# Four products in four PSUM banks, narrow products, and unread products in the edge layers of a four-layer graph kernel

## The chip, the cores and the metric

The kernel runs on one core of a Trainium2 chip. The core has a matrix engine (PE), a vector engine (DVE), a scalar engine (ACT), a general engine (POOL, which here issues the gathers), and SP, which issues DMAs. The metric is the device time of one execution in microseconds, the median of several runs. PE's granted clock is given as a share of 2.4 GHz: a stretch shows a mean between 0.5 (1.2 GHz) and 1.0.

## What is computed

A graph of 100,000 nodes with 16 features each and 50,000 edges goes through four layers. `h` is the layer norm of `x` with a relu, `src` and `dst` the ends of the edges:

```python
h = relu(layernorm(x)); x = x + L0(h)   # messages h[src] * edge weight * w0, summed by dst
h = relu(layernorm(x)); x = x + L1(h)   # msg = sum_k t[:, k] * (h[dst] @ W[k]), 16 terms, summed by src
h = relu(layernorm(x)); x = x + L2(h)   # two edge convolutions, 16 inputs x 8 outputs x 9 edge terms each
                                        # (two own layer norms), plus h @ Wr + bias for every node ("root")
h = relu(layernorm(x)); x = x + L3(h)   # m = silu(einsum('ei,ej,ijh->eh', h[dst], attr8, Wmsg)) @ Wlin, summed by src;
                                        # then for every node silu(einsum('ni,nh,ihk->nk', h, agg, Wupd)) @ Wulin + h
```

## The kernel before

The edges are first sorted by block of nodes (a block is 14 columns of nodes) into records in DRAM, once by `dst` (`edges_by_dst`) and once by `src` (`edges_by_src`); POOL writes them with `place`. A layer's edges are 448 tiles of 128 edges, 8 tiles make a group (`G`), so a layer has 56 groups; in the code a group is `group(i, k)`, `g = i * RING + k`, with four buffers for rows and records (`RING`). A node stage between layers adds the sums to `x` and writes the next `h` to a table. At the end seven chunks of an update work through all nodes.

What happens to a group `g` in layers 1, 2 and 3:

- SP fetches its records, POOL gathers its rows of the table (8 indirect DMAs, line 464, one for each tile).
- PE transposes the rows (line 587), ACT copies the transpose to `featT` (line 780; in layer 2 twice, with two gains, line 777). In `featT` the 8 tiles' 16 features lie in 8 bands of 16 partitions.
- PE multiplies `featT` by a block-diagonal weight matrix: four products in layers 1 (512 columns) and 2 (288 columns), two in layer 3 (512 columns), at line 560. Each product concerns only two tiles (32 partitions) in layer 1 and four tiles (64 partitions) in layers 2 and 3; the other rows of its columns are zeros. Two PSUM banks, `psP`, take the products in turn, so product 2 waits for DVE's multiplication 0 and product 3 for multiplication 1.
- DVE multiplies each product by the edge's terms (lines 1155, 1168, 1183), reduces (1160, 1176, 1188), and spreads the messages over the columns of their block (`spread_out`, line 1112). In layer 2, PE also computes the "root" products of a part of the nodes (line 576), DVE waits for them before it reduces, as they lie in the bank where it writes, and adds them to `x` at the group's end (1212, 1214).
- PE sums the edges of group `g - 1` by node: eight products, one for each tile, of 224 columns (line 551), into `psK`, 4 banks of two tiles each. DVE adds them up in a running sum (`run`, line 1130), eight steps, each with the one before as input. The sums come in halves of four: DVE waits for four, PE for the running sums of the same tiles of the group before.
- SP writes the running sums to DRAM (`keep_run`) and fetches the records for group `g + 4`.

PE executes in the order in which the code is written: transpose, four products, (root products), eight sums of the group before. In layer 1, six products that nobody reads (`ident` times part of `W3`, line 595) stand between products 1 and 2. Layer 0 has no products; DVE scales the rows (1139, 1143).

DVE's order in a group is: the terms and the block columns (1148, 1107), the multiplications, the reduction, the spreading, the running sums of the group before. In layer 3 the running sums stand before the spreading, while ACT computes the silu.

In the update (line 653) PE makes, for each quad of nodes, two products of 512 columns in the two halves of `psQ[q % 2]`; DVE multiplies them (1265) and reduces what POOL has halved (1258, 495). Three times a chunk PE also transposes or multiplies for the chunk's other steps (618, 624, 630). A float32 product shows as two records of MATMUL in the trace.

Of the kernel before, what the change touches and what calls it, by code (L numbers as in the profile page):

```python
# [4 lines left out]
P = 128  # L5
# [67 lines left out]
def build_gnn(nc, x_in, src_in, dst_in, attr2_in, attr8_in, attr8_rev_in, ew_in, w0_in, slw_in, w1_in,  # L73
# [10 lines left out]
    with ctx:  # L84
# [118 lines left out]
        psR = psX[:, 1536:2048]  # L203
        raw = [psR[:, 256 + i * P:256 + (i + 1) * P] for i in range(2)]
# [297 lines left out]
        def _(pe):  # L502
# [22 lines left out]

            for l in range(4):
# [3 lines left out]
                if l == 1:  # L530
                    parts = [(0, W1[:, m * 512:(m + 1) * 512]) for m in range(4)]
                elif l == 2:
                    parts = [(s, W2[s][:, q * 288:(q + 1) * 288]) for s in range(2) for q in range(2)]
                elif l == 3:
                    parts = [(0, W3[:, m * 512:(m + 1) * 512]) for m in range(2)]
                else:
                    parts = []
                n = len(parts)

                def sums(i, k, half, first=False):  # L540

                    q = i * RING + (k - 1)
                    par = (k - 1) % 2
# [5 lines left out]
                    for t in range(4 * half, 4 * half + 4):  # L549
                        o = t // 2 * 512 + t % 2 * BW  # L550
                        nc.tensor.matmul(psK[:, o:o + BW], at_lo[par][:, t * P:(t + 1) * P],  # L551
                                         spread[par][:, t * BW:(t + 1) * BW], start=True, stop=True)\
                            .then_inc(e["summed"], 1)

                def product(i, k, m, first):
                    g = i * RING + k
                    s, w = parts[m]
                    if m >= 2 or not first:
                        pe.wait_ge(e["used"], g * n + (m - 1))
                    nc.tensor.matmul(psP[m % 2][:, 0:w.shape[1]], featT[:, s * P:(s + 1) * P], w,  # L560
# [20 lines left out]
                def group(i, k, first=False, second=False):  # L581
                    g = i * RING + k
                    if l:
# [6 lines left out]
                        for m in range(n):  # L590
                            product(i, k, m, first)
                            if l == 1 and m == 1:

                                for _ in range(6):
                                    nc.tensor.matmul(psT[:, 256:512], ident[:, :], W3[:, 0:256], start=True, stop=True)
                        if l == 2:
                            root_products(i, k, first)
                    if not first:
                        sums(i, k, 0, second)
                        sums(i, k, 1, second)  # L600

# [32 lines left out]
            def step(c, first, last_one):  # L634
                for q in range(QUADS):
# [15 lines left out]
                    for j in range(2):  # L651
                        b, m = q // 2, 2 * (q % 2) + j
                        k = nc.tensor.matmul(psQ[q % 2][:, j * 512:(j + 1) * 512], rt[:, b * P:(b + 1) * P],  # L653
# [662 lines left out]
```

## Time and profile before

| | us |
|---|---|
| median of 3 runs | 4295.58 |
| lowest and highest | 4289.64, 4299.15 |
| the profiled execution | 4291.38 |
| its span on the core | 4289.6 |

The profile gives the busy time of each engine, the idle time of an engine before an instruction with what ended it ("waited for"), and the chain of work that ended last. "issue" is time in which an engine waited for nothing that the profile shows. In the table by stage the engines' busy times come first, with their counts of instructions, then PE's granted clock, the share of DMA time and GB/s. PEld is PE's loading of weights. In a row of the trace an operation is named by its line, its kind, what it writes and reads, and the number of instructions merged in the row ("x16"); behind it in brackets stands the idle time before it and what ended it. Names drop the numbers of buffers.

### The profile page before, as it was taken

Reading aid. Unit: us, or ns where it says so; the run is one execution under the profiler, and the core shown is the slowest. Engines: PE = TensorE matmul, PEld = TensorE weight load, DVE = VectorE, ACT = ScalarE, POOL = GpSimd, SP = SyncE. Lnnn points to the kernel's source line nnn. Section 1 sums busy time; section 2 is a strip of 40 time slices with the busy share of each in tenths; the row PEclk is TensorE's granted clock in tenths of the full one; section 3 lists DMA queues with packets and bytes.
Section 4 is the critical chain, followed back from the end, with each engine's and each line's share of the span. In section 5 each row is a group of like instructions: output and inputs, shape, how many; then the busy total and the mean of one; then the engine's idle time right before and its main releaser. Section 6 shows DMA issues by size and latency. Waiting matters only on the chain.

```text
span 4289.6 us, 28738 instructions
## 1 busy us (share of the span) xinstructions
PE 2171.9 (51%) x7442; PEld 1517.8 (35%) x7442; DVE 2886.2 (67%) x4329; ACT 1192.7 (28%) x2949; POOL 2739.8 (64%) x2799
## 2 busy tenths in 40 slices
PE   1200035545300005888887046667651666767998
PEld 1100024444300003555555035555540444444444
DVE  8892036666570005888888867777767888877887
ACT  1000023333420003333343234444422433430110
POOL 3777777777777777655653056666622777764776
PEclk7555567777655557999999568888875888889999
DMA  6011023333630001222223322222343333351110
GB/s 178 9 31 46 8 59 109 110 102 109 101 101 5 5 5 45 83 83 79 87 83 86 98 69 91 90 89 83 90 95 111 107 98 107 107 95 43 35 35 26
DMA packets 200521, 321.19 MB, mean 75 GB/s; under 512 B 83898, under 2 KB 166698, under 8 KB 199971
## 3 DMA queue, kind: packets, MB, share of 16 engines
q1 hardware_dynamic: 112848, 265.61, 17.3%
q0 software_dynamic: 82368, 21.64, 7.7%
q10 hardware_dynamic: 5140, 32.09, 2.0%
q8 instruction: 60, 0.98, 0.1%
q14 instruction: 105, 0.86, 0.1%
HBM read 66.90 MB, written 252.21 MB: 74 GB/s over the span
## 4 chain that ended last, share of the span: by engine, by line
POOL 38%; DVE 23%; issue 19%; PE 17%; DMA 1%; SPq 1%; ACT 0%; DVEq 0%; POOLq 0%
POOL rows L464 20%; DVE work L1130 9%; POOL edges_by_dst L448 9%; POOL edges_by_src L448 9%; PE psX L653 7%; PE psX L560 6%; DVE psX L1160 3%; DVE natD L1155 2%; DVE psX L1176 2%; PE psX L576 2%; DVE h L1020 1%; PE psK L551 1%; DVE psX L1017 1%; PE psK L630 1%; DVE x L1214 0%
## 5 line engine op out<-in xcount | busy, mean ns | idle before, releaser
L464 POOL DMA_INDIRECT rows<-table,rec x1792 | 1693.0, 945 | 1087.1 <-issue 519.2
L551 PE MATMUL psK<-work 128*128 128x224 f32 x3584 | 896.1, 413 | 576.5 <-DVE work L1112 298.1
L551 PEld LDWEIGHTS psK<-work 128*128 128x128 f32 x3584 | 822.1, 234 | 719.7 <-issue 666.4
L1130 DVE SCALAR_TENSOR_TENSOR work<-work,keep,psK 128x224 f32<-128x224 f32 x1792 | 800.9, 447 | 87.3 <-PE psK L551 15.9
L560 PE MATMUL psX<-natD 128*128 128x512 f32 (+1 forms) x1120 | 608.4, 678 | 340.4 <-DVE natD L1168 150.0
L760 ACT ACTIVATE work<-iota,rec 128x128 f32<-128x128 f32 x1792 | 545.9, 391 | 576.2 <-PE psK L551 358.9
L448 POOL DMA_INDIRECT edges_by_dst<-natD,pos x391 | 374.7, 958 | 184.2 <-issue 127.0
L1112 DVE TENSOR_TENSOR work<-at_hi,psX 128x1792 f32<-128x1792 f32 x224 | 452.2, 2019 | 6.1 <-ACT psX L802 0.3
L448 POOL DMA_INDIRECT edges_by_src<-natS,pos x391 | 374.4, 958 | 128.1 <-issue 128.1
L587 PE MATMUL psX<-ident,rows 128*128 128x128 f32 x168 | 51.6, 307 | 767.3 <-DMA rows<-table,rec 767.3
L560 PEld LDWEIGHTS psX<-natD 128*128 128x128 f32 x1120 | 231.4, 229 | 556.5 <-DVE natD L1168 176.3
L653 PE MATMUL psX<-natD,work 128*128 128x512 f32 x784 | 339.9, 592 | 1.0 <-ACT work L838 1.0
L495 POOL TENSOR_TENSOR work<-natS 128x512 f32<-128x512 f32 x196 | 244.6, 1262 | 129.7 <-DVE natS L1265 129.4
L780 ACT ACTIVATE natD<-psX 128x128 f32<-128x128 f32 x112 | 31.1, 278 | 1048.8 <-PE psX L587 1048.8
L587 PEld LDWEIGHTS psX<-ident,rows 128*128 128x128 f32 x168 | 24.3, 145 | 790.1 <-issue 496.8
L1139 DVE TENSOR_TENSOR psX<-rows,rec 128x128 f32<-128x128 f32 x56 | 17.0, 303 | 426.3 <-DMA rows<-table,rec 426.3
L1265 DVE TENSOR_TENSOR natS<-psX,h 128x1024 f32<-128x1024 f32 x196 | 237.9, 1214 | 56.0 <-PE psX L653 56.0
L1148 DVE TENSOR_TENSOR natD<-hats 128x128 f32<-128x128 f32 x56 | 15.9, 284 | 379.6 <-ACT hats L751 379.6
L764 ACT ACTIVATE work<-work,one 128x1024 f32<-128x1024 f32 x224 | 257.1, 1148 | 7.3
L653 PEld LDWEIGHTS psX<-natD,work 128*128 128x128 f32 x784 | 145.0, 189 | 182.4 <-issue 109.8
L1155 DVE TENSOR_TENSOR natD<-psX,natD 128x512 f32<-128x512 f32 x224 | 149.7, 689 | 77.5 <-PE psX L560 75.6
L1168 DVE TENSOR_TENSOR natD<-psX,rec 128x288 f32<-128x288 f32 x224 | 97.1, 453 | 92.4 <-PE psX L560 92.2
(147 smaller groups left out, 2342.6 us busy)
## 6 DMA issues: line engine op xcount, KB each, us to landing
scan<-work SPq DMA_DIRECT2D x224, 896.0 KB
rows<-table,rec POOLq DMA_INDIRECT x1792
table<-h ACTq DMA_DIRECT2D x28, 896.0 KB, 3.6
work<-scan SPq DMA_DIRECT2D x168, 112.0 KB, 2.0
rec<-edges_by_dst SPq DMA_DIRECT2D x112, 84.0 KB, 1.9
natD<-scan SPq DMA_DIRECT2D x56, 112.0 KB, 2.0
edges_by_dst<-natD,pos POOLq DMA_INDIRECT x391
edges_by_src<-natS,pos POOLq DMA_INDIRECT x391
```

Source lines behind the costliest of these rows:

```text
L448: pool.indirect_dma_start(out=rec_by[s].ap(), out_offset=bass.IndirectOffsetOnAxis(ap=pos[s][0:n, u:u + 1], axis=0), in_=nat[0:n, u * F:(u ...
L464: pool.indirect_dma_start(out=rows[k][:, u * D:(u + 1) * D], out_offset=None, in_=table.ap(), in_offset=bass.IndirectOffsetOnAxis(ap=rec[k ...
L495: nc.gpsimd.tensor_tensor(hf, w[:, :, :, 0:8], w[:, :, :, 8:16], ALU.add).then_inc(up["half"], 1)
L551: nc.tensor.matmul(psK[:, o:o + BW], at_lo[par][:, t * P:(t + 1) * P], spread[par][:, t * BW:(t + 1) * BW], start=True, stop=True)\
L560: nc.tensor.matmul(psP[m % 2][:, 0:w.shape[1]], featT[:, s * P:(s + 1) * P], w, start=True, stop=True).then_inc(e["prod"], 1)
L653: k = nc.tensor.matmul(psQ[q % 2][:, j * 512:(j + 1) * 512], rt[:, b * P:(b + 1) * P], W4[:, m * 512:(m + 1) * 512], start=True, stop=True)
L760: a = S.activation(at_lo[par][:, t * P:(t + 1) * P], iota1[:, :], ACT.Abs, bias=field(l, k, LO[ORDER[l]])[:, t, :])
L764: S.activation(at_lo[par], at_lo[par], ACT.Relu, scale=-1.0, bias=one[:, :]).then_inc(e["lo"], 1)
L1112: V.tensor_tensor(spread[par].rearrange("p (u c f) -> p u c f", c=BC, f=D), v3(at_hi[par][:, :], BC)[:, :, :, None].to_broadcast([P, G, BC ...
L1130: V.scalar_tensor_tensor(acc[par][:, t * BW:(t + 1) * BW], was, keep[s][:, bass.ds(q * G + t, 1)], psK[:, o:o + BW], ALU.mult, ALU.add).th ...
L1155: V.tensor_tensor(prod[:, m * 512:(m + 1) * 512].rearrange("p (u o k) -> p u o k", o=D, k=D), psP[m % 2].rearrange("p (u o k) -> p u o k", ...
L1265: V.tensor_tensor(products(q)[0], psQ[q % 2].rearrange("p (u k i) -> p u k i", k=D, i=D), v3(h[:, bass.ds(c * CW + 64 * q, 64)])[:, :, Non ...
```

## The change

Four things are done.

1. In layers 1 and 2 products 2 and 3 go to the first two banks of `psK` (where the sums of tiles 0 to 3 lie) instead of `psP`. On PE the sums of tiles 4 to 7 now stand before those of tiles 0 to 3, and the latter wait, two by two, for DVE's multiplications 2 and 3. In layer 2 the root products stand between the two halves. DVE's running sums wait once for all eight sums in these two layers.
2. Each product reads only the partitions of `featT` and of the weights that count: 32 in layer 1, 64 in layers 2 and 3, and 32 in the final update.
3. Unread products (`spin`): four in layer 1, at the end of a group instead of six between products; four between the halves of the sums and six behind them in layers 0 and 3. Layer 2 has none.
4. Product 0 and 1 of a group wait for multiplications 0 and 1 of the group before.

```diff
+        product_at = psP + [psK[:, 0:512], psK[:, 512:1024]]
...
+            def spin(n):
+                for _ in range(n):
+                    nc.tensor.matmul(psT[:, 256:512], ident[:, :], keep[0][:, 0:256], start=True, stop=True)
...
-                    parts = [(0, W1[:, m * 512:(m + 1) * 512]) for m in range(4)]
+                    parts = [(0, 32 * m, 32, W1[:, m * 512:(m + 1) * 512]) for m in range(4)]
...
-                    parts = [(s, W2[s][:, q * 288:(q + 1) * 288]) for s in range(2) for q in range(2)]
+                    parts = [(s, 64 * q, 64, W2[s][:, q * 288:(q + 1) * 288]) for s in range(2) for q in range(2)]
...
-                    parts = [(0, W3[:, m * 512:(m + 1) * 512]) for m in range(2)]
+                    parts = [(0, 64 * m, 64, W3[:, m * 512:(m + 1) * 512]) for m in range(2)]
...
+                def late_product(g, m):
+                    s, row, high, w = parts[m]
+                    if g == 1:
+                        pe.wait_ge(e["used"], m + 1)
+                    elif g > 1:
+                        pe.wait_ge(e["run"], (g - 2) * G + 2 * (m - 1))
+                    nc.tensor.matmul(psK[:, (m - 2) * 512:(m - 2) * 512 + w.shape[1]],
+                                     featT[row:row + high, s * P:(s + 1) * P], w[row:row + high, :],
+                                     start=True, stop=True).then_inc(e["prod"], 1)
+                def upper_sums(g):
+                    pe.wait_ge(e["spread"], g)
+                    pe.wait_ge(e["lo"], g)
+                    if g > 1:
+                        pe.wait_ge(e["run"], (g - 1) * G)
+                    sums_of(g - 1, range(4, 8))
+                def lower_sums(g):
+                    for b in range(2):
+                        pe.wait_ge(e["used"], g * n + 3 + b)
+                        sums_of(g - 1, (2 * b, 2 * b + 1))
...
-                    if m >= 2 or not first:
-                        pe.wait_ge(e["used"], g * n + (m - 1))
+                    if not first:
+                        pe.wait_ge(e["used"], (g - 1) * n + (m + 1))
...
-                        for m in range(n):
+                        for m in range(2):
                             product(i, k, m, first)
-                            if l == 1 and m == 1:
-                                for _ in range(6):
-                                    nc.tensor.matmul(psT[:, 256:512], ident[:, :], W3[:, 0:256], start=True, stop=True)
+                    if n == 4:
+                        for m in range(2, 4):
+                            late_product(g, m)
+                        if not first:
+                            upper_sums(g)
                         if l == 2:
                             root_products(i, k, first)
-                    if not first:
+                        if not first:
+                            lower_sums(g)
+                        if l == 1:
+                            spin(4)
+                    elif not first:
                         sums(i, k, 0, second)
+                        spin(4)
                         sums(i, k, 1, second)
+                        spin(6)
...
-                        k = nc.tensor.matmul(psQ[q % 2][:, j * 512:(j + 1) * 512], rt[:, b * P:(b + 1) * P],
-                                             W4[:, m * 512:(m + 1) * 512], start=True, stop=True)
+                        two = slice(32 * m, 32 * m + 32)
+                        k = nc.tensor.matmul(psQ[q % 2][:, j * 512:(j + 1) * 512], rt[two, b * P:(b + 1) * P],
+                                             W4[two, m * 512:(m + 1) * 512], start=True, stop=True)
...
-                        if t % 4 == 0:
+                        if l in (1, 2):
+                            if t == 0:
+                                dve.wait_ge(e["summed"], q * G + G)
+                        elif t % 4 == 0:
                             dve.wait_ge(e["summed"], q * G + (t + 4))
```

DVE's multiplications read `product_at[m]` instead of `psP[m % 2]`.

PE in layer 1, one group in the middle of the layer, before. `psK<-work` are the sums, `psX<-natD` the products, `ident` with 256 columns the unread ones; in brackets the semaphores that a row waits for (`used` counts DVE's multiplications, `run` its running sums).

```order
L587 MATMUL psX<-ident,rows 128x128 [waits gath3]
L560 MATMUL psX<-natD 128x512 [waits e1_used,e1_bandS]
L560 MATMUL psX<-natD 128x512 [waits e1_used]
L595 MATMUL psX<-natD,ident 128x256 x6
L560 MATMUL psX<-natD 128x512 [waits e1_used] x2
L551 MATMUL psK<-work 128x224 [waits e1_run,e1_lo,e1_spread]
L551 MATMUL psK<-work 128x224 x3
L551 MATMUL psK<-work 128x224 [waits e1_run]
L551 MATMUL psK<-work 128x224 x3
```

The same group's place in the changed kernel:

```order
L623 MATMUL psX<-ident,rows 128x128 [waits gath0]
L595 MATMUL psX<-natD 128x512 [waits e1_used,e1_bandS]
L595 MATMUL psX<-natD 128x512 [waits e1_used]
L571 MATMUL psK<-natD 128x512 [waits e1_run] x2
L550 MATMUL psK<-work 128x224 [waits e1_run,e1_lo,e1_spread]
L550 MATMUL psK<-work 128x224 x3
L550 MATMUL psK<-work 128x224 [waits e1_used]
L550 MATMUL psK<-work 128x224
L550 MATMUL psK<-work 128x224 [waits e1_used]
L550 MATMUL psK<-work 128x224
L530 MATMUL psX<-keep,ident 128x256 x4
```

The wait for `used` has moved from products 2 and 3 to the last four sums, and products 2 and 3 wait for `run`.

PE in layer 2, one group before (`root` products are the 128 x 128 ones behind the products):

```order
L587 MATMUL psX<-ident,rows 128x128
L560 MATMUL psX<-natD 128x288 [waits e2_used,e2_bandS]
L560 MATMUL psX<-natD 128x288 [waits e2_used] x3
L576 MATMUL psX<-natD 128x128 [waits r_added,r_rowsS]
L576 MATMUL psX<-natD 128x128 x3
L551 MATMUL psK<-work 128x224 [waits e2_run,e2_lo,e2_spread]
L551 MATMUL psK<-work 128x224 x3
L551 MATMUL psK<-work 128x224 [waits e2_run]
L551 MATMUL psK<-work 128x224 x3
```

And in the changed kernel:

```order
L623 MATMUL psX<-ident,rows 128x128
L595 MATMUL psX<-natD 128x288 [waits e2_used,e2_bandS]
L595 MATMUL psX<-natD 128x288 [waits e2_used]
L571 MATMUL psK<-natD 128x288 [waits e2_run] x2
L550 MATMUL psK<-work 128x224 [waits e2_run,e2_lo,e2_spread]
L550 MATMUL psK<-work 128x224 x3
L612 MATMUL psX<-natD 128x128 [waits r_added,r_rowsS]
L612 MATMUL psX<-natD 128x128 x3
L550 MATMUL psK<-work 128x224 [waits e2_used]
L550 MATMUL psK<-work 128x224
L550 MATMUL psK<-work 128x224 [waits e2_used]
L550 MATMUL psK<-work 128x224
```

The root products now follow four sums, which wait for the end of the running sums before.

## Rows read from the trace of the kernel before

**Rows 1.** The page: the chain that ended last, by engine and by line.

```profile
POOL 38%; DVE 23%; issue 19%; PE 17%; DMA 1%; SPq 1%; ACT 0%; DVEq 0%; POOLq 0%
POOL rows L464 20%; DVE work L1130 9%; POOL edges_by_dst L448 9%; POOL edges_by_src L448 9%; PE psX L653 7%; PE psX L560 6%; DVE psX L1160 3%; DVE natD L1155 2%; DVE psX L1176 2%; PE psX L576 2%; DVE h L1020 1%; PE psK L551 1%; DVE psX L1017 1%; PE psK L630 1%; DVE x L1214 0%
```

**Rows 2.** Layers 0 to 3, update: PE, PEld, DVE, ACT, POOL busy (x); PEclk, DMA.

```profile
580.00:1137.00 557.00, 288.98 (x880) 248.87 (x880) 336.10 (x652) 204.14 (x522) 421.39 (x446) 0.72 0.39 103
1645.00:2350.00 705.00, 581.18 (x2065) 397.59 (x2064) 605.62 (x890) 274.19 (x835) 412.58 (x438) 0.94 0.28 80
2518.00:3187.00 669.00, 465.74 (x1871) 385.38 (x1871) 523.76 (x997) 297.50 (x769) 407.64 (x431) 0.81 0.31 88
3301.00:3874.00 573.00, 383.09 (x1171) 254.09 (x1171) 458.59 (x726) 223.33 (x607) 411.09 (x436) 0.83 0.37 100
3888.00:4284.00 396.00, 385.57 (x1176) 193.55 (x1176) 342.08 (x393) 47.67 (x41) 295.26 (x209) 0.98 0.10 28
```

**Rows 3.** Who waited for whom in layer 1: us, times, longest.

```profile
DVE natD L1155 <- PE psX L560: 75.6, 114, 3.1
```

**Rows 4.** Layer 1's first operation of a group on DVE: ns, first and last start.

```profile
L1148 DVE TENSOR_TENSOR natD<-hats x56: 282/283/293, 1645.2 to 2336.8; 128x128 f32<-128x128 f32 x56
```

**Rows 5.** Timeline of layer 1: start, duration, operation, [idle time before it].

```profile
2066.95 3.19 PE L551 MATMUL psK<-work 128*128 128x224 f32 x16
...
2072.44 2.75 PE L595 MATMUL psX<-natD,ident 128*128 128x256 f32 x12
...
2077.20 2.50 PE L560 MATMUL psX<-natD 128*128 128x512 f32 x4 [2.01 <-DVE natD L1155]
...
2079.74 0.69 DVE L1155 TENSOR_TENSOR natD<-psX,natD 128x512 f32<-128x512 f32 x1 [0.69 <-PE psX L560]
...
2084.73 3.89 DVE L1130 SCALAR_TENSOR_TENSOR work<-work,keep,psK 128x224 f32<-128x224 f32 x8
```

**Rows 6.** Who waited for whom in layer 2.

```profile
DVE natD L1168 <- PE psX L560: 72.7, 103, 1.1
...
DVE psX L1176 <- PE psX L576: 50.6, 55, 1.3
```

**Rows 7.** Layer 2's reductions on DVE, two a group.

```profile
L1176 DVE TENSOR_REDUCE psX<-natD x112: 748/756/761, 2515.7 to 3178.1; 128x64 f32<-128x576 f32 x112
```

**Rows 8.** Timeline of layer 2, two groups one after the other.

```profile
2702.21 1.24 PE L560 MATMUL psX<-natD 128*128 128x288 f32 x4 [1.66 <-DVE natD L1168]
...
2703.28 1.05 PE L576 MATMUL psX<-natD 128*128 128x128 f32 x8
...
2704.44 1.42 DVE L1176 TENSOR_REDUCE psX<-natD 128x64 f32<-128x576 f32 x2 [0.50 <-PE psX L576]
...
2707.83 3.89 DVE L1130 SCALAR_TENSOR_TENSOR work<-work,keep,psK 128x224 f32<-128x224 f32 x8
...
2713.12 2.04 PE L560 MATMUL psX<-natD 128*128 128x288 f32 x4 [3.29 <-DVE natD L1168]
...
2716.97 1.42 DVE L1176 TENSOR_REDUCE psX<-natD 128x64 f32<-128x576 f32 x2 [1.32 <-PE psX L576]
```

**Rows 9.** Timeline of layer 3, POOL: two gathers, eight apart.

```profile
3520.28 0.94 POOL L464 DMA_INDIRECT rows<-table,rec  x1 [0.30 <-issue]
...
3530.26 0.94 POOL L464 DMA_INDIRECT rows<-table,rec  x1 [0.30 <-issue]
```

**Rows 10.** Who waited for whom in the final update.

```profile
DVE natS L1265 <- PE psX L653: 56.0, 22, 20.3
```

**Rows 11.** The chain of work in the update: start, us, engine and line.

```profile
3974.03 30.91 PE psX L653 x72
...
4028.30 30.91 PE psX L653 x72
```

**Rows 12.** Timeline of the update, DVE: two multiplications, one quad apart.

```profile
4031.79 1.21 DVE L1265 TENSOR_TENSOR natS<-psX,h 128x1024 f32<-128x1024 f32 x1
...
4033.51 1.21 DVE L1265 TENSOR_TENSOR natS<-psX,h 128x1024 f32<-128x1024 f32 x1
```

More of the change, by code:

```diff
@@ L538, in _, with sums_of @@
                 n = len(parts)
+                def sums_of(q, tiles):
+                    par = q % 2
+                    for t in tiles:
+                        o = t // 2 * 512 + t % 2 * BW
+                        nc.tensor.matmul(psK[:, o:o + BW], at_lo[par][:, t * P:(t + 1) * P],
+                                         spread[par][:, t * BW:(t + 1) * BW], start=True, stop=True)\
+                            .then_inc(e["summed"], 1)
                 def sums(i, k, half, first=False):
                     q = i * RING + (k - 1)
-                    par = (k - 1) % 2
                     if half == 0:
@@ L548, in sums @@
                         pe.wait_ge(e["run"], q * G + (4 * half + 4 - G))
[L549 to L553, printed above, removed]
+                    sums_of(q, range(4 * half, 4 * half + 4))
+                def late_product(g, m):
[17 more added lines that the diff above has]
+                        sums_of(g - 1, (2 * b, 2 * b + 1))
                 def product(i, k, m, first):
                     g = i * RING + k
-                    s, w = parts[m]
-                    if m >= 2 or not first:
-                        pe.wait_ge(e["used"], g * n + (m - 1))
-                    nc.tensor.matmul(psP[m % 2][:, 0:w.shape[1]], featT[:, s * P:(s + 1) * P], w,
+                    s, row, high, w = parts[m]
+                    if not first:
+                        pe.wait_ge(e["used"], (g - 1) * n + (m + 1))
+                    nc.tensor.matmul(psP[m % 2][:, 0:w.shape[1]], featT[row:row + high, s * P:(s + 1) * P],
+                                     w[row:row + high, :],
                                      start=True, stop=True).then_inc(e["prod"], 1)
@@ L1155, in messages @@
                             V.tensor_tensor(prod[:, m * 512:(m + 1) * 512].rearrange("p (u o k) -> p u o k", o=D, k=D),
-                                            psP[m % 2].rearrange("p (u o k) -> p u o k", o=D, k=D),
+                                            product_at[m].rearrange("p (u o k) -> p u o k", o=D, k=D),
                                             v3(basis)[:, 2 * m:2 * m + 2, None, :].to_broadcast([P, 2, D, D]),
@@ L1169, in messages @@
                                             .rearrange("p (u o t) -> p u o t", o=HALF, t=A9),
-                                            psP[m % 2][:, 0:288].rearrange("p (u o t) -> p u o t", o=HALF, t=A9),
+                                            product_at[m][:, 0:288].rearrange("p (u o t) -> p u o t", o=HALF, t=A9),
                                             at.to_broadcast([P, 4, HALF, A9]), ALU.mult).then_inc(e["used"], 1)
```

## The prediction

> **What bounds the kernel now.** I read the chain of work first [rows 1]: POOL holds 38% of it, DVE 23%, PE 17%, so no one engine is the kernel's limit and each stage has to be read alone. The busy time by stage [rows 2] gives five stretches: layer 0's edges, layers 1, 2 and 3's edges, and the final update. What is left out between them (sorting, placing edges, node stages) the change doesn't touch.
>
> Layer 1. A group takes 12.57 us (the first operation of a group runs 56 times from 1645.2 to 2336.8: 691.6 / 55) [rows 4]. DVE is busy 86% of the stretch, POOL 59% [rows 2]. DVE's only large wait is for products, 75.6 us [rows 3], less 3 us or so at the first group, 1.31 us a group. One group shows it [rows 5]: product 2 may not start before DVE has freed the bank of product 0, so PE stands idle 2.01 us, issues products 2 and 3 at 2077.20, and DVE idles before each of its last two multiplications, 0.69 us before the last. Without the waits a group is 12.57 - 1.31 = 11.26 us of DVE work.
>
> Layer 2. A group takes 12.03 us: its two reductions run from 2515.7 to 3178.1, less 0.7 us between the two of a group, over 55 [rows 7]. DVE waits 72.7 us for products and 50.6 us for the root sums that stand behind them on PE [rows 6], together 2.24 us a group, which leaves 9.79 us. The clock has a part in it: the stretch ran at 0.81 of full speed, so about 38% of the time at 1.2 GHz and the rest at 2.4 [rows 2]. PE idled 3.29 us before products 2 and 3, they then ran at half speed (2.04 us, against 1.24 at full speed in the group before), and DVE waited 1.32 us for the root sums, against 0.50 us in that group before [rows 8].
>
> Layers 0 and 3. POOL issues gathers without a break: eight of them, one group, from 3520.28 to 3530.26, so 9.98 us [rows 9]. It is POOL that sets these layers, at 0.72 and 0.83 of PE's clock [rows 2]; behind layer 0, POOL goes on with placing edges by source (9% of the chain) [rows 1], for which no other engine is needed.
>
> Final update. PE is on the chain: 72 products' records in 30.91 us, 0.429 us each, 1.72 us for the four of a quad, and between them bursts for transposes and the step's small products; a chunk takes 4028.30 - 3974.03 = 54.27 us [rows 11]. DVE's own pace is the same 1.72 us a quad with no idle time between [rows 12], 28 x 1.72 = 48.2 us a chunk, so the other 6 us are DVE's waits: 56.0 us in all, 20.3 of them the first one [rows 10], leaving 36 us.
>
> **The change, part by part.**
>
> *Products 2 and 3 in other banks, layer 1.* They no longer wait for multiplications 0 and 1 of the same group but for the running sums of tiles 0 to 3 of two groups back, which end on DVE before the group begins. So all four products should lie ready, and 1.31 us a group goes. What is late next: the sums of tiles 0 to 3 now stand behind multiplications 2 and 3, and DVE waits for all eight sums where it waited for four and four. That wait has cover: the reduction and the spreading lie between, and in the group shown 2084.73 - 2079.74 = 5.0 us pass from the start of multiplication 3 to the first running sum [rows 5], while the lower four sums take about 1.5 us at 2.4 GHz (half of the 3.19 us of all eight [rows 5]) and under 3.5 at 1.2. Behind PE's waits are queued only its own next sums and, after them, the next group's transpose, wanted some 7 us later. ACT's columns and SP's refills wait for counts that come no later than now. Bounds: 73 us (56 x 1.31) and, should half of the waits come back through a slower clock, 37. I take a period of 11.35 us, near the first end because the work left on PE fits: 56 x (12.57 - 11.35) = **-68 us**.
>
> *The same in layer 2.* Products 2 and 3 leave the multiplications' shadow, and the root products now stand behind the upper four sums, which wait for the end of the previous running sums. From the end of the running sums PE then needs, at full clock, 1.6 us for four sums (half of 3.19 [rows 5]) and 1.05 us for the root products [rows 8], 2.65 us. DVE is busy meanwhile with the root additions, the block columns and four multiplications: of its 9.79 us a group the reductions, the spreading and the running sums take 2707.83 + 3.89 - 2704.44 = 7.28 [rows 8], so 2.5 us are left for these. So 0.1 to 0.4 us of the 2.24 stay at 2.4 GHz (0.4 where the group before had fewer root blocks to add); at 1.2 GHz PE's 2.65 become 5.3, and some 2.5 us stay. DVE without idle time is 9.79 us, POOL 9.98 us: POOL becomes the floor. For the clock: PE's longest gap is now 3.29 us, in layer 1 it is 2.01, and that layer ran at 0.94 against 0.81 [rows 2, 5, 8]. In the new order I find PE's gaps (waiting for tile pairs, for the end of the run, for multiplications) at 1.5 us or less, so a clock like layer 1's. Bounds: a period of 10.0 us gives 56 x 2.03 = 114 us; the clock staying at 0.81 gives about 10.9 us (38% of the groups with 2.5 us, the others with 0.3), 63. I take 10.35: 56 x 1.68 = **-94 us**.
>
> *Unread products.* Layer 1 goes from six to four, in a place where PE waits anyway: nothing. Layers 0 and 3 get ten a group. Six take 2.75 us at full clock [rows 5], ten 4.6. In layer 0 they come to eight sums (about 3.0 us): 7.6 of 9.98 us, hidden by POOL's gathers. In layer 3 it is tight: sums, transpose, copy and two products take 2072.44 - 2066.95 = 5.49 us, ten unread products about 4.35 us back to back: 9.84 us against POOL's 9.98 [rows 5, 9]. If the clock drops as in layer 1 (0.94) it is some 10.4 us, +0.4 x 56 = 24 us. Bounds 0 and +30; I take **+5 us**, since a PE without idle time ran at the full clock in the final stage (0.98) [rows 2].
>
> *Products that read only 32 or 64 rows.* No row shows such a product at work beside another. If it streams as long as now, nothing changes; if two of a quad overlap, PE ceases to bind the update and DVE's pace stays, at most -36 us [rows 10, 12]. The bursts remain (54.27 - 28 x 1.72 = 6.1 us a chunk), and DVE would still wait at some. I take **-15 us**, between the ends and nearer to none, since nothing in the rows shows an overlap. By a page of the Trainium skill (TensorE: Matmul & The Clock Gate, Part 3) products whose operands start in different row groups run concurrently, four of 32 rows measured at 3.07 times the speed; by that the term would be -20 to -36. No run here shows it yet. Against the change speaks another page (TensorEngine Tiling (Array Packing), Key Properties): a change of tiling mode drains TensorE. Each group of layers 1 to 3 would have two changes; at 0.17 us each, an estimate from the time by which a pair of products lasts longer than the distance to what follows it (1.24 against 2703.28 - 2702.21 = 1.07 us [rows 8]), they would be hidden in layers 1 and 2 and would take layer 3 from 9.84 to 10.18 us, +11 us.
>
> *DVE, ACT, POOL, SP* execute the same instructions, except for fewer waits: nothing.
>
> **Sum.** -68 - 94 + 5 - 15 = -172 us. The profiled execution took 4291.4 us (span 4289.6), so 4119.4; it lies 4.2 us under the median of 4295.6, so 4124 for the median.
>
> **Rivals.**
>
> A. *The narrow products gain nothing, and layer 3 turns to PE.* For it: no row shows an overlap, and layer 3's margin is 0.14 us a group. Time: the update term 0, layer 3 +20: 4124 + 15 + 15 = 4154. It is also the case in which this part of the change doesn't do what it says.
>
> B. *The clock doesn't recover.* Layer 2 stays near 0.81 and its root sums stay late: -63 instead of -94, layer 1 -50 instead of -68: 4124 + 49 = 4173. For it: the share of time in which PE streams falls if products overlap. Against it: the gaps get shorter.
>
> C. *Slower than before.* PE's clock in the final update falls from full to half, because PE works on a quarter of its rows or because overlapped products leave it idle half the time. Its place is the 196 quads, where 1.72 us of PE work would be 3.43: 196 x 1.71 = 335 us, and without the 15 us gained there, 4124 + 15 + 335 = about 4474. It turns slower than before when the update loses more than the 157 us that the layers gain, 157 / 196 = 0.80 us a quad, so at a mean clock under about 0.7 there. Against it: the stretch is at 0.98 with PE the limit [rows 2], and a PE that becomes slow becomes busy again.
>
> **How the numbers follow.** Forecast case 0.60, centre 4124, with its own unknowns from 4124 - 20 (layer 2 at 10.0) - 21 (update at full gain) = about 4083 up to 4160. A 0.20, B 0.12, C 0.05, others 0.03. To hold eight times in ten the range takes in A and B and the errors about them: 4080 to 4200. A difference under 0.2% (8.6 us) is about what a measurement of this kernel can't tell from none. Faster by more: all of the forecast, A and B and most of the rest, 0.93; the same 0.02; slower 0.05.
>
> **What would show it.** In the new profile: DVE's wait for products in layer 1 near zero and its group at 11.3 us; DVE's wait for root sums in layer 2 under 0.5 us a group, the stretch's clock at 0.9 or more, POOL without waits for records; layer 3's group still 10 us with PE near 100% busy at clock 1.0; in the update, a chunk of 50 to 52 us and PE below 90% busy if products overlap, 54 us and 100% if not. I would be wrong if DVE found the eight sums late (a new wait before the running sums), if layer 2's clock stayed at 0.8, or if the narrow products ran at 1.2 GHz.

## The result

The changed kernel takes 4223.26 us (median of 4, 4222.88 to 4223.82) against 4295.55: ratio 0.983, 95% interval 0.9816 to 0.9843. It is 72 us faster, where 172 were forecast, and lies outside the range of 4080 to 4200.

The profile after, first the shares of the chain of work, from the page of the changed kernel:

```profile
POOL 38%; DVE 24%; issue 19%; PE 15%; ACT 2%; DMA 1%; SPq 1%; POOLq 0%; DVEq 0%
```

They have hardly moved against [rows 1], and don't tell where the time went. So the stages of the changed kernel, with the columns of [rows 2]: the stretch, busy times of PE, PEld, DVE, ACT, POOL, then PE's clock. The rows are layers 1, 2, 3 and the update, each cut to where it now lies.

```profile
1645.00:2270.00 625.00, 539.29 (x1849) 375.12 (x1849) 599.38 (x899) 275.09 (x839) 413.51 (x439) 0.82 0.33 92
2430.00:3090.00 660.00, 479.65 (x1855) 369.99 (x1855) 509.05 (x985) 297.31 (x769) 408.87 (x433) 0.78 0.32 88
3215.00:3787.00 572.00, 505.93 (x2271) 404.29 (x2271) 451.42 (x724) 221.94 (x605) 409.14 (x434) 0.97 0.38 102
3810.00:4216.00 406.00, 352.42 (x1140) 150.86 (x1138) 336.73 (x388) 45.94 (x39) 289.19 (x205) 0.63 0.09 25
```

PE's clock has gone from 0.94 to 0.82 in layer 1, from 0.81 to 0.78 in layer 2 and from 0.98 to 0.63 in the update; where ten unread products a group were put in, it has risen, in layer 3 from 0.83 to 0.97 and in layer 0 from 0.72 to 0.93.

The same operations of the changed kernel as in [rows 4] and [rows 7], and the update's multiplications, grouped by line with mean durations and the first and last start; under the second, who it waited for (us in all, times):

```profile
L1196 DVE TENSOR_TENSOR natD<-hats x56: 283/283/291, 1646.1 to 2252.1; 128x128 f32<-128x128 f32 x56
```

```profile
L1224 DVE TENSOR_REDUCE psX<-natD x112: 749/756/762, 2428.8 to 3087.1; 128x64 f32<-128x576 f32 x112
...
  PE psX L612: 132.3, 56
```

```profile
L1313 DVE TENSOR_TENSOR natS<-psX,h x196: 1210/1214/1226, 3802.8 to 4197.5; 128x1024 f32<-128x1024 f32 x196
```

A group of layer 1 takes (2252.1 - 1646.1) / 55 = 11.02 us instead of 12.57. A group of layer 2 takes (3087.1 - 0.7 - 2428.8) / 55 = 11.96 instead of 12.03: DVE no longer waits for products, but the wait for root sums has grown from 51 to 132 us, 2.36 us a group. The update's multiplications span 394.7 us; before it was 372.2.

The marks between the stages, first for the kernel before, then for the changed one:

```profile
L1188 DVE TENSOR_REDUCE natD<-natD x56: 1219/1220/1221, 3301.6 to 3859.3; 128x128 f32<-128x1024 f32 x56
L1265 DVE TENSOR_TENSOR natS<-psX,h x196: 1205/1212/1226, 3894.2 to 4266.4; 128x1024 f32<-128x1024 f32 x196
...
L1236 DVE TENSOR_REDUCE natD<-natD x56: 1219/1220/1222, 3212.6 to 3769.1; 128x128 f32<-128x1024 f32 x56
```

From the first start in each stage the sum closes: layer 1 up to layer 2's first reduction took 870.5 us (1645.2 to 2515.7), now 782.7, so -88; from there to layer 3's first reduction 785.9, now 783.8, so -2; layer 3 up to the update 592.6, now 590.2, so -2; the update to the end of the span 395.4, now 418.3, so +23; and +1 before all of them. Together -68 of span.

Layer 1 in the trace of the changed kernel, one group, PE and DVE (columns as in [rows 5]):

```profile
2071.96 1.13 PE L595 MATMUL psX<-natD 32*128 32x512 f32 x4 [0.37 <-ACT natD L824]
...
2072.84 2.09 PE L571 MATMUL psK<-natD 32*128 32x512 f32 x4
...
2075.83 4.65 PE L550 MATMUL psK<-work 128*128 128x224 f32 x16 [0.90 <-DVE work L1178]
...
2076.11 1.29 DVE L1203 TENSOR_TENSOR natD<-psX,natD 128x512 f32<-128x512 f32 x2
...
2077.31 1.28 DVE L1203 TENSOR_TENSOR natD<-psK,natD 128x512 f32<-128x512 f32 x2
...
2078.62 2.29 DVE L1208 TENSOR_REDUCE psX<-natD 128x128 f32<-128x2048 f32 x1
```

No DVE row has idle time in brackets. Two products of 32 rows take 1.13 us. Two of 128 rows took 1.98 in the kernel before:

```profile
2084.37 1.98 PE L560 MATMUL psX<-natD 128*128 128x512 f32 x4 [0.37 <-ACT natD L780]
```

So neighbouring narrow products do overlap. The Trainium skill (TensorE: Matmul & The Clock Gate, Part 3) says that products in different row groups run concurrently; the trace agrees, with 1.13 us against 1.98. But the eight sums, which read all rows, took 4.65 us here. In the kernel before, most groups took the 3.19 of [rows 5], some more (4.40 in the next group); the stretch's mean clock fell from 0.94 to 0.82.

Layer 2 of the same trace, where that hurts, in the same columns. `L550` are the sums, here the upper four (8 records), `L612` the root products:

```profile
2771.76 3.33 PE L550 MATMUL psK<-work 128*128 128x224 f32 x8 [1.28 <-DVE work L1178]
...
2774.88 1.10 PE L612 MATMUL psX<-natD 128*128 128x128 f32 x8
...
2776.09 1.42 DVE L1224 TENSOR_REDUCE psX<-natD 128x64 f32<-128x576 f32 x2 [2.04 <-PE psX L612]
```

The upper sums start as soon as the running sums end, take 3.33 us instead of the 1.6 of my sum, and the reduction waits 2.04 us for what stands behind them. It is so in every group of this trace between 2505 and 2790 us: the upper sums take 3.2 or 3.3 us.

### The profile page after: what moved, and what is told of

Same layout as the page of the kernel before. It is cut to its first block, busy times and chain, and to the rows that moved or that the text cites. A ratio compares the mean times of both kernels' runs of the same rounds, so it can differ in the third digit from the quotient of the medians.

```text
span 4221.1 us, 32578 instructions
## 1 busy us (share of the span) xinstructions
PE 2403.8 (57%) x9418; PEld 1742.2 (41%) x9418; DVE 2860.9 (68%) x4329; ACT 1192.4 (28%) x2949; POOL 2737.7 (65%) x2799
## 4 chain that ended last, share of the span: by engine, by line
POOL 38%; DVE 24%; issue 19%; PE 15%; ACT 2%; DMA 1%; SPq 1%; POOLq 0%; DVEq 0%
POOL rows L465 20%; POOL edges_by_dst L449 9%; POOL edges_by_src L449 9%; DVE work L1178 8%; PE psK L550 5%; PE psX L697 5%; DVE natD L1203 3%; DVE psX L1208 3%; PE psX L612 2%; DVE natS L1313 2%; DVE psX L1224 1%; PE psK L673 1%; ACT work L804 1%; DVE h L1064 1%; DMA rows<-table,rec 1%
## 5 line engine op out<-in xcount | busy, mean ns | idle before, releaser
L550 PE MATMUL psK<-work 128*128 128x224 f32 x3584 | 972.9, 429 | 520.4 <-DVE work L1156 292.5
L550 PEld LDWEIGHTS psK<-work 128*128 128x128 f32 x3584 | 814.9, 236 | 707.9 <-issue 649.1
L530 PE MATMUL psX<-keep,ident 128*128 128x256 f32 x2648 | 634.2, 387 | 0.0
L530 PEld LDWEIGHTS psX<-keep,ident 128*128 128x128 f32 x2648 | 519.1, 196 | 62.2 <-issue 1.5
L697 PE MATMUL psX<-natD,work 32*128 32x512 f32 x784 | 283.2, 963 | 46.3 <-DVE natS L1313 45.3
L571 PE MATMUL psK<-natD 32*128 32x512 f32 (+1 forms) x448 | 210.5, 602 | 69.0 <-DVE work L1178 68.8
L595 PE MATMUL psX<-natD 32*128 32x512 f32 (+2 forms) x672 | 174.6, 597 | 91.3 <-ACT natD L821 50.2
L697 PEld LDWEIGHTS psX<-natD,work 32*128 32x128 f32 x784 | 79.7, 268 | 224.3 <-DVE natS L1313 202.3
```

The source lines that it names most:

```text
L530: nc.tensor.matmul(psT[:, 256:512], ident[:, :], keep[0][:, 0:256], start=True, stop=True)
L571: nc.tensor.matmul(psK[:, (m - 2) * 512:(m - 2) * 512 + w.shape[1]], featT[row:row + high, s * P:(s + 1) * P], w[row:row + high, :], start ...
```

## The experiments

Three sets were run, each on one chip with the kernel before beside it. "Group" is layer 2's group, from the reductions; "update" is the time from the first to the last of the update's 196 multiplications. The expectations set two theories against each other. Theory 1: narrow products lower PE's clock, and the clock holds layer 2 and the update back. Theory 2: in layer 2 it is the place of the root products behind the upper sums, whatever the clock.

| kernel | us | group of layer 1 | group of layer 2 | update |
|---|---|---|---|---|
| before | 4296 | 12.57 | 12.03 | 372.2 |
| changed | 4223 | 11.02 | 11.96 | 394.7 |
| changed, again | 4222 | 11.02 | 11.92 | 394.8 |
| narrow products alone | 4280 | 12.05 | 11.95 | 394.6 |
| root products first | 4126 | 11.02 | 10.19 | 397.3 |
| full products in layer 2 and update | 4107 | 11.02 | 10.28 | 372.2 |
| both of these | 4106 | 11.02 | 10.18 | 372.2 |
| full products everywhere | 4113 | 11.01 | 10.24 | 372.3 |
| no unread products in layers 0 and 3 | 4228 | 11.02 | 11.92 | 396.7 |
| update: one full unread product a quad | 4215 | 11.02 | 10.17 | 494.2 |

### First set: engines that stall

In this set the kernel before took 4925 us. The traces have a kind of idle time that the others lack, here from the kernel with full products everywhere (who waited for whom: us, times, longest):

```profile
DVE work L1178 <- remote: 1175.8, 92, 53.5
```

What an engine waits for there the profile doesn't say, and whether it belongs to the chip or to its state at the time isn't shown. The times of whole kernels, and of the layers, don't bear on the question of the clock. The update is free of such waits in these traces, so I read it alone. Yet one thing in the whole times is not explained: here the changed kernel with full products in the update took 1.025 times as long as the kernel before, and with full products everywhere 1.058, while narrow products alone took 0.996. Whether the changed program suffers more from the stalls was not tested, so its gain is shown only where engines don't stall.

Full products in the update alone:

```diff
-                        two = slice(32 * m, 32 * m + 32)
+                        two = slice(0, P)
```

> The changed kernel with the products of the final update alone over all 128 rows again. Both theories: the stretch of the update returns from 418 to 395 us with clock 1.0, nothing else moves: 4200 us. If the update lost its 23 us to something else than the narrow products, it stays at 4223.

5051 us in this set, ratio 1.025; the update's multiplications span 373.0 us at clock 1.0, here in the middle of the update:

```profile
4700.00:5000.00 300.00, 300.00 (x908) 147.24 (x907) 271.36 (x314) 36.27 (x31) 239.79 (x167) 1.00 0.10 31
```

For the update this is as expected, so its loss is the narrow products'.

Full products everywhere (`parts` with rows 0 to 127 in each entry, and the edit above):

> The changed kernel with every product over all 128 rows again, in the layers and in the update; banks, order and unread products stay as changed. Theory 1 (narrow products lower PE's clock, and the clock is what holds layer 2 and the update back): update chunk back from 58.0 to 54.3 us at clock 1.0 (-23 us), layer 2's group from 11.96 to 10.8 us or less at a clock over 0.85 (-60), layer 1 at 11.0 us as now: about 4135 us. Theory 2 (in layer 2 the root products' place behind the upper sums is what holds it, whatever the clock): layer 2 stays at 11.9, only the update returns: about 4200 us.

5219 us, ratio 1.058; the update 372.3 us at clock 1.0; the layers can't be read, so this kernel comes again in the third set.

Narrow products alone, on the kernel before (the `row, high` slices of the diff, and `two`, with nothing else):

> The kernel before with narrow products alone (32 and 64 rows in the layers, 32 in the update). Theory 1: the update loses 23 us as in the changed kernel, and the clock of layers 1 to 3 falls, so DVE's waits for products grow: 4320 to 4350 us. Rival (narrow products are harmless in the layers, since a pair takes 1.13 instead of 1.98 us): layers gain 10 to 20 us, sum with the update 4295 to 4310.

4897 us, ratio 0.9957 (0.9917 to 0.9998). The update spans 373.8 us, no longer than with full products, though at clock 0.67. The same kernel took 394.6 us for it in the third set, so the loss in the update doesn't belong to the program alone; this is taken up below.

Both products of a quad read rows 0 to 31. Its update computes other values; the number and size of its instructions are those of the changed kernel.

```diff
-                        two = slice(32 * m, 32 * m + 32)
+                        two = slice(0, 32)
```

> The changed kernel, but in the update both products of every quad read rows 0 to 31, whatever their tiles (so the update's values are others; the amount of work is the same). No two neighbouring products then lie in different rows. If it is idle time left by overlapping products that lowers the clock in the update: no overlap, PE busy nearly all the time, clock 1.0, chunk 54.3 us, about 4200 us. If it is the small number of rows: clock at 0.5 with 3.4 us of PE work a quad, some 300 us more, about 4520 us.

The stages' table of this kernel, over the update:

```profile
4639.00:5310.00 671.00, 670.02 (x1116) 294.01 (x1114) 351.83 (x388) 43.31 (x37) 294.61 (x208) 0.56 0.06 16
```

The whole takes 5354 us (two runs), the update's multiplications 670.1 us. PE is busy 670 of 671 us and its clock stays at 0.56, most of the time at 1.2 GHz; a quad takes 3.41 us, so two products in the same rows don't overlap. Full products, as busy, get 1.0. So it is not idle time that lowers the clock in the update, it is that only 32 rows work. This decided the question that rival C had left open ("a quarter of its rows or ... idle half the time") for the former.

### Second set: what holds layer 2

> The changed kernel once more, beside the variants of this set on one chip, as their yardstick: ratio to before 0.983 on the chip of the first measurement. The first set of experiments ran on a chip where the engines stalled for several us at a time and before itself took 4925 us. If the change's gain belongs to the program, the ratio is again 0.98; if the 1976 additional PE records cost time there through fetching instructions, it is nearer 1.0 or above on such a chip.

4221.8 us, ratio 0.9828 (0.9808 to 0.9847): the first result again, on runs free of stalls. What additional records cost where engines stall, as the expectation asks, it can't say.

Root products ahead of the upper sums:

```diff
-                        if not first:
-                            upper_sums(g)
                         if l == 2:
                             root_products(i, k, first)
+                        if not first:
+                            upper_sums(g)
```

> The changed kernel with layer 2's root products ahead of the upper four sums. Theory 1 (what holds layer 2 is PE at half clock, with its place in the order only saying who shows it): DVE no longer waits for root sums but for the eight sums, and a group stays above 11 us: 4185 to 4220 us. Theory 2 (the order holds it): the wait goes, a group takes 10.1 us: 4223 - 56 x 1.85 = 4120 us.

4125.7 us (4110 to 4135), ratio 0.9597 (0.9558 to 0.9635). The group takes 10.19 us with the products still narrow. Theory 1, which had named the clock alone, is refuted for layer 2. Layer 2 of this kernel in the stages' table:

```profile
2430.00:2990.00 560.00, 396.51 (x1841) 317.43 (x1839) 509.45 (x982) 296.85 (x768) 413.50 (x437) 0.83 0.40 102
```

There PE's clock is 0.83. In its timeline the root products, still slow in this group, come in time, and all eight sums behind them are done before DVE has reduced and spread:

```profile
2757.41 0.44 PE L602 MATMUL psX<-ident,natD 128*128 128x128 f32 x2 [2.23 <-DMA rows<-table,rec]
...
2770.93 1.85 PE L612 MATMUL psX<-natD 128*128 128x128 f32 x8
...
2772.62 3.19 PE L550 MATMUL psK<-work 128*128 128x224 f32 x16
...
2772.89 1.42 DVE L1224 TENSOR_REDUCE psX<-natD 128x64 f32<-128x576 f32 x2 [0.39 <-PE psX L612]
```

The first row says who sets the pace now: PE waits for rows, and POOL gathers eight of them in 10.0 us without a break.

Full products in layer 2 and in the update, the order as changed (`parts = [(s, 0, P, W2...)]`, and `two = slice(0, P)`):

> The changed kernel with layer 2's products and the update's over all 128 rows; the order stays. The kernel in which the update's products all read rows 0 to 31 showed PE 100% busy at a clock of 0.56: it is the rows that lower the clock. Theory 1 then expects in layer 2 a clock of 0.9, root sums 0.3 us late instead of 2.4 and a group of 10.3 us; with the update's 21 us: 4223 - 21 - 90 = 4112 us. Theory 2: clock may rise, the group stays near 11.9: 4200 us.

4107.5 us, ratio 0.9568 (0.9543 to 0.9593). The group takes 10.28 us at clock 0.96; layer 2 in the stages' table and in the timeline of this kernel:

```profile
2430.00:2990.00 560.00, 401.87 (x1837) 305.24 (x1836) 500.27 (x970) 295.56 (x764) 414.04 (x437) 0.96 0.38 102
```

```profile
2773.21 1.05 PE L612 MATMUL psX<-natD 128*128 128x128 f32 x8
...
2774.10 1.68 PE L550 MATMUL psK<-work 128*128 128x224 f32 x8
...
2774.37 1.42 DVE L1224 TENSOR_REDUCE psX<-natD 128x64 f32<-128x576 f32 x2 [0.46 <-PE psX L612]
```

Root products and lower sums run at full clock and the reduction waits 0.46 us. So theory 2, which had named the order alone, is refuted too.

Both edits together:

> Both edits: root products first and full products in layer 2, full products in the update. Theory 1: as the kernel with full products alone, a little less (10.0 to 10.3 us a group), 4100 to 4112 us. Theory 2: the same 4100 us, and the gain over full products alone is 90 us.

4106.3 us (4101 to 4109), ratio 0.9555 (0.9536 to 0.9573), 2.7% faster than the changed kernel beside it and no different, within the runs' scatter, from full products alone (4107 to 4120). The group takes 10.18 us, 0.1 less than with full products alone and the same as with the order alone.

The four corners (narrow or full, root products behind or ahead) are 11.92, 10.28, 10.19 and 10.18 us. Neither the clock nor the order costs more than 0.1 us by itself. PE at half clock has some 2.4 us (the wait per group) too much work between the end of the running sums and the reduction; move the four sums out of that stretch, or double the clock, and it fits.

### Third set: the parts one by one

Narrow products alone, again:

> The kernel before with narrow products alone, again, since its first run fell on the chip with stalls (there the update took 373.8 us from first to last multiplication at clock 0.69, as long as with full products, against 394.7 at 0.63 in the changed kernel). If the narrow products cost the update 22 us by themselves: update 395 us; with clocks of 0.8 in layers 1 and 2 more waiting for products there: 4320 to 4340 us. If the loss needs what else was changed: update 373 us and 4290 to 4300 us.

4280.2 us, ratio 0.9935 (0.9907 to 0.9963). Layers 1 and 2, and the update of this kernel in the stages' table:

```profile
1645.00:2350.00 705.00, 567.85 (x2074) 391.09 (x2074) 615.04 (x907) 275.97 (x841) 416.40 (x440) 0.88 0.30 85
2518.00:3187.00 669.00, 440.20 (x1799) 354.05 (x1799) 513.88 (x975) 287.33 (x740) 389.27 (x411) 0.78 0.33 91
...
3888.00:4280.00 392.00, 338.55 (x1110) 146.77 (x1106) 322.75 (x372) 45.95 (x39) 279.73 (x198) 0.63 0.09 26
```

Against my expectation they gain in layer 1: 0.52 us a group, 29 us, as products 2 and 3, on DVE's path there, overlap. Layer 2 gains 0.08 us a group, at a lower clock, and the update loses 22 us, as in the changed kernel. In sum that is 11 us, and the medians differ by 22, with single runs from 4265 to 4287. So narrow products are a gain where two of them stand on the path and a loss where full-width work follows them on it.

Full products everywhere, again (same kernel as in the first set):

> The changed kernel with full products everywhere, on a chip without stalls. Layer 2 and the update as in the kernel with full products there alone (10.3 us a group, 372 us). In question: layer 1, where narrow products run at clock 0.82 and DVE has no waits (11.02 us a group). If layer 1 is DVE's alone, it stays 11.0 with a clock over 0.9; layer 3 with full products: PE needs 9.84 us a group by my sum against POOL's 9.98, so 10.0 to 10.3 us: 4107 to 4125 us. If the narrow rows were of use in layer 1 or 3, 4130 or more.

4113.5 us, ratio 0.9558 (0.9536 to 0.9580), inside the expected 4107 to 4125. Its layers 1, 2 and 3 in the stages' table:

```profile
1645.00:2270.00 625.00, 523.63 (x1849) 327.99 (x1849) 598.85 (x897) 275.06 (x839) 413.49 (x439) 0.99 0.33 92
2430.00:2990.00 560.00, 404.39 (x1840) 307.70 (x1839) 502.89 (x972) 295.82 (x768) 411.73 (x434) 0.96 0.39 102
3130.00:3690.00 560.00, 530.33 (x2264) 423.34 (x2263) 451.87 (x715) 219.68 (x598) 405.28 (x429) 0.99 0.38 102
```

In layer 1 the clock goes from 0.82 to 0.99 and the group stays at 11.01 us: layer 1 is DVE's alone, as predicted. Layer 3, where by my sum PE needs 9.84 us a group against POOL's 9.98, indeed has PE busy 95% and still takes (3680.0 - 3122.2) / 55 = 10.14 us a group, as before.

No unread products in layers 0 and 3 (the calls `spin(4)` and `spin(6)` there taken out):

> The changed kernel without the unread products of layers 0 and 3. If they only raise the clock there, while POOL sets the pace: layer 0 and 3 take the same time (556 us each from first to last group), clock back to 0.72 and 0.75: 4223 us +- 5. If they delay anything, it gets faster by up to 10 us; if the clock was of use in layer 3's last groups, slower by up to 10.

4228.2 us, ratio 0.9826 (0.9804 to 0.9848), the same as with them. Layer 3 in its stages' table:

```profile
3215.00:3787.00 572.00, 356.97 (x1168) 247.04 (x1169) 453.10 (x720) 222.89 (x607) 411.56 (x435) 0.80 0.37 100
```

0.80 against 0.97, and its 55 groups take 560.1 us instead of 556.5. With unread products the same layer took 556.5 to 561.5 us in the other traces, so the unread products raise the clock as they should, and it buys nothing measurable.

A full unread product to hold the clock in a narrow update (root products first and full products in layer 2):

```diff
+                    nc.tensor.matmul(psQ[q % 2][:, 0:128], ident[:, :], keep[0][:, 0:128], start=True, stop=True)
                     for j in range(2):
```

> Root products first and full products in layer 2; the update with narrow products and, ahead of each quad's two, one unread product over 128 rows and 128 columns. If the clock follows the rows at work, it rises from 0.63; at 0.8 or more, DVE's waits fall under 56 us and the update from 394.7 to 350 to 372 us: 4085 to 4106 us. If one full product of eight does not raise it, PE has more work at half clock: 410 us, 4140 us.

4214.8 us (4174 to 4228), with the update at 494 us, longer than in every version but the one whose products all read rows 0 to 31; the update in the stages' table:

```profile
3720.00:4200.00 480.00, 472.98 (x1476) 210.56 (x1475) 338.70 (x380) 43.32 (x37) 288.25 (x203) 0.65 0.07 21
```

The mean clock stayed at 0.65. In the stretches at half clock (0.50 from 3910 to 3940 us) a quad took 2.73 us against 1.75: the added product itself 0.7, and the two narrow ones 2.0, as they still overlap each other but no longer the next quad's. The expectation's second branch held in sign, but its price (410 us) was far too low.

## Why the prediction was wrong, step by step

Four terms made -172 us; -68 came. Layer 2 missed by 92 us and the update by 38, and layer 1 and layer 3 gave 20 and 7 us more than forecast.

**What bounds each layer** was right: every version in which neither products nor root sums are late has a group of 11.0 us in layer 1, where DVE has hardly any idle time, and 10.2 to 10.3 us in layer 2, where POOL's 9.98 us is close and, with the root products first, sets the pace. Only the 11.26 us for layer 1 was too high.

**Layer 1, -68 us: right in mechanism, 20 us too small.** The waits for products are gone, the wait for eight sums found the predicted cover, and the gain was 88 us. The term that was mis-sized is "without the waits a group is 11.26 us". The group is 11.02: an operation that waits costs more than the idle time in brackets. Before, the four multiplications took 4.01 us from first start to the reduction (2076.45 to 2080.46), of which 1.31 in brackets; now they take 2078.62 - 2076.11 = 2.51 us, 0.19 less than the difference (without a wait a multiplication starts 0.1 us before the record of the one before ends, as 2076.11 + 1.29 against 2077.31). Most of the rest is the running sums, 3.82 us where they took 3.89. I had also left 0.09 us for waits that never came back.

**Layer 2, -94 us: wrong, -2 us.** The step that failed is "In the new order I find PE's gaps ... at 1.5 us or less, so a clock like layer 1's". The gaps are as short as I said (1.28 us before the upper sums), but layer 1's own clock fell to 0.82 and layer 2's to 0.78, as the products became narrow. I had judged the clock by idle gaps alone and treated the narrow products as a matter of the update. Full products in the same order, with the same gap of 1.27 us there, bring layer 2 back to 0.96: it was the narrow products, not that gap. The arithmetic behind it was right: I wrote that at 1.2 GHz "some 2.5 us stay", and 2.36 us stayed. Wrong was the weight: with a clock of 0.8 I had let 38% of the groups run slow, while in fact the upper sums, which come right after the narrow products and a gap, ran at half clock in group after group (3.2 or 3.3 us in each of the 24 groups between 2505 and 2790 us). That is also why the lower bound (-63) didn't hold. Rival B had the direction ("the clock doesn't recover") with 0.12, and my bound for it was too mild by the same step.

**Unread products, +5 us: right, nothing.** The sum of 9.84 us for PE against 9.98 for POOL held even with full products; the drain that a change of tiling mode costs by the Trainium skill (TensorEngine Tiling (Array Packing), Key Properties) did not come out in any group's time: layer 3 took 10.12 us a group with narrow products and 10.14 with full ones. As PE was busy only 506 of 572 us with the narrow ones, a short drain could hide there.

**Narrow products in the update, -15 us: wrong in sign, +23 us.** The overlap took place. What I counted only as rival C, the clock falling "because PE works on a quarter of its rows", took place as well, and its price was far below my 335 us, since the two partly cancel. Where nothing overlaps (both products in rows 0 to 31) it was 670.1 - 373.0 = 297 us. The chain of the changed kernel (start, us, line) over one chunk, to be held against [rows 11]:

```profile
4011.58 22.80 PE psX L697 x52
4034.38 3.18 PE psK L667 x14
...
4043.93 5.35 PE psK L673 x28
...
4059.00 3.05 PE psK L661 x14
...
4069.61 1.22 PE psX L697
```

Thirteen quads of overlapped narrow products take 22.80 us, 1.75 us each: at half clock, overlapped, they are as fast as full products at full clock. The loss lies in the three bursts, which read all rows: 3.18, 5.35 and 3.05 us, together 11.6. In the kernel before:

```profile
4004.94 1.53 PE psK L624 x14
...
4013.34 3.12 PE psK L630 x28
...
4026.77 1.53 PE psK L618 x14
```

That is 6.2 us together. So a chunk loses 5.4 us in the bursts and gains 1.6 in the other quads: it is 4069.61 - 4011.58 = 58.03 us, 3.8 more than before, and the six distances between the first and the last of seven chunks make the 394.7 - 372.2 = 22.5 us.

The narrow update of the first set, which lost nothing, differs mostly in that; a row of its chain:

```profile
4571.39 3.32 PE psK L630 x28
```

There the burst of 28 ran at full clock, 2.0 us shorter, and its chunk was 4594.75 - 4540.13 = 54.6 us; of the other 1.4 us, 1.1 lie in the quads just before that burst, also at full clock (0.98), and 0.3 in the last burst. Where within a chunk the clock rises thus decides over 3 us; why it rose there and not in the five other traces with this update, one of them of the same kernel, is open.

**What stays open.** That narrow rows lower the clock is shown for 32 rows in the update, where nothing but the rows differs from the full products that ran at 1.0. Why the clock follows the rows, no run shows. For 64 rows in layer 2 it is shown that full products raise the clock from 0.78 to 0.96 in the same order, but not how much of it is rows and how much the shorter time in which narrow products keep PE at work.

## What to carry to other kernels

Before narrowing a product to the rows that count, look at what follows it on the matrix engine: the narrow ones may overlap and lose nothing, but full-width work behind them may run at the clock that they leave. A sum for a stretch of waits has to be made at both clock levels, and if it fits at only one of them, move work out of the stretch rather than hope for the clock: here the order alone brought 96 us. And judge a clock by what rows were at work before, not by gaps alone.

## What was not expected of the hardware

- PE 100% busy with products of 32 rows, none of them overlapping, had a mean clock of 0.56; full products in the same place 1.0.
- Two neighbouring products of 32 rows and 512 columns took 1.13 us, two full ones 1.98, both at full clock; full ones need 1.72 us a quad back to back, narrow ones at half clock and overlapped 1.75.
- Taking 1.31 us of waits out of a group saved 1.55 us: a multiplication that waits costs about 0.1 us beyond its idle time (two a group, 0.19 us), and the running sums became 0.07 us shorter.
- In one set engines were held for up to 53.5 us at a time on DVE with no cause in the profile, and the same kernel took 15% longer.
